# Layer 1's attention on one core: three runs of value products a group for seven, and the side products beside them

## The chip, the core and the metric

The kernel runs on one core of a Trainium2 chip. The metric is device time in microseconds, the median of several runs; lower is better.

## What is computed

Four layers, each a cross attention and then a feed-forward part, on x (8 x 256 x 128) with a context of 8 x 1601 x 128. The change touches layer 1's cross attention alone, 16 heads of width 8:

```python
q = query @ Wq + bq          # query: layernorm(x)
k = key @ Wk + bk            # key, value: the context
v = value @ Wv + bv
scores = jnp.einsum('bqhd,bkhd->bhqk', q, k) * scale
attn = jax.nn.softmax(scores, axis=-1)
out = jnp.einsum('bhqk,bkhd->bqhd', attn, v)
return out.reshape(out.shape[0], out.shape[1], ATTEN_DIM) @ Wo + bo
```

## The kernel before

`build_heads` works in bodies, one for each of the 8 batch elements, and a body in 4 groups of 4 heads (`NG`). The context's 1601 positions are 13 tiles of 128 (`CT`). For a group there are:

- 14 **top** steps (T0 to T13 of a numbering in which 4 to 13 are done one group ahead, as `T`, and 0 to 3 two groups ahead, as `U`): PE multiplies queries and keys (line 454) into a PSUM tile of the ring, and DVE takes maxima over positions (lines 717, 715). Steps 12 and 13 are narrow (66 columns).
- **shift** (`H`), three small operations on DVE that turn the maxima into a row, and **rows** (`W`), a product of PE (line 501) with DVE's addition (line 731): they put the maximum into `shifted`, so that the next group's scores come out less their maximum.
- 13 **score** steps (S0 to S12): PE (line 435) into a ring tile, ACT takes the exponential into `probs` (line 603), which has 8 places (`PS`).
- 7 **value** steps (V0 to V6) of two tiles each, the last of one: PE adds probabilities times values into `res` (line 475), four products of 32 columns a tile, one a head. **Result** (`R`) is ACT's copy of `res` into `oraw` (line 607).

`ring` has 3 tiles of two banks each (`RING`); scores and tops take them in turn, and PE waits for the one three ring steps back to be read. One more bank, `aux`, serves the **side products**, placed by the table `SIDE`: key (line 487, the next body's, copied by ACT at line 617 and subtracted by DVE at 739), value (line 492, the projection of the next body's values, copied by ACT at 625), denominator (line 511), spread (521, read by DVE at 748), project (527) and finish (534) for the body before.

The order of everything is written by hand: `ORDER` is a string with one group's steps, `SIDE` says after which step of which group (0 to 3) a side product stands and for which body, and every engine walks the same list (`run_bodies`) with its own part of each step. Offsets in the list say that a step belongs to the group before or after. A product in 64 rows (scores, tops), one in 128 rows and 32 columns (values) and one in 128 by 128 (`aux`) are three shapes of the array, named 64*128, 128*32 and 128*128 in the trace.

Of the kernel before, what the change touches and what calls it, by code (L numbers as in the profile page):

```python
# [59 lines left out]
class Semaphores:  # L60
# [3 lines left out]
    def __init__(self, nc):  # L64
        self.nc = nc
        self.old, self.now, self.later = [(ExitStack(), []) for _ in range(3)]
# [113 lines left out]
class HeadsPlan:  # L180
# [3 lines left out]
    H, DH, NG, HG = 16, 8, 4, 4  # L184
# [8 lines left out]
    KB = -(-CT // 4)  # L193
    AUX = ("key", "value", "rows", "denominator", "spread", "project", "finish")

    ORDER = """S0 T4 S1 V5 T12 S2 T13 T5 V6 S3 T6 R T7 S4 T8 V0 S5 T9 V1 T10 S6 T11 V2 S7 U0 U1 H S8 S9 V3 U2 S10 W S11 U3 S12 V4"""
    SIDE = {(0, "T4"): ("key", 0, 1), (0, "T7"): ("key", 1, 1), (0, "T9"): ("key", 2, 1), (0, "T11"): ("key", 3, 1),
            (0, "V3"): ("denominator", 0, -1), (1, "S1"): ("spread", 0, -1), (1, "T13"): ("spread", 1, -1), (1, "T6"): ("project", 0, -1),
            (1, "U0"): ("value", 0, 1), (2, "S4"): ("finish", 0, -1), (2, "U0"): ("value", 1, 1), (3, "R"): ("value", 2, 1),
            (3, "U0"): ("value", 3, 1)}  # L200

    def __init__(self):

        self.order = []
        put = lambda kind, n, off=0: self.order.append((kind, off, n))
        for g in range(self.NG):
            of = lambda d: ((g + d) % self.NG, (g + d) // self.NG)
            for s in self.ORDER.split():  # L210
                k = int(s[1:] or 0)
                if s[0] == "S":
                    put("scores", g * CT + k)
                elif s[0] in "TU":
                    G, off = of(1 if s[0] == "T" else 2)
                    put("tops", (G, k), off)
                elif s[0] == "H":
                    put("shift", *of(1))
                elif s[0] == "W":
                    put("rows", *of(1))  # L220
                elif s[0] == "V":
                    G, off = of(-1 if k >= 5 else 0)
                    put("values", G * self.PV + k, off)
                else:
                    put("result", *of(-1))
                if (g, s) in self.SIDE:
                    put(*self.SIDE[g, s])
        self.aux = Numbered(self.order, self.AUX, ("key",))
        self.ring = Numbered(self.order, ("scores", "tops"))
        self.high = Numbered(self.order, ("key",), ("key",))  # L230


def build_heads(nc, held, io, x, x_in, x_out):
    c = HeadsPlan()
# [3 lines left out]
    with ExitStack() as ctx, ExitStack() as done:  # L238
# [56 lines left out]
        aux_full, aux_free, hi_ok, parts_ok = sem("aux_full"), sem("aux_free"), sem("hi_ok"), sem("parts_ok")  # L295
# [245 lines left out]
        def _(act):  # L541
# [62 lines left out]

            def result(b, par, g):
                act.wait_ge(pv_ok, b * NG * c.PV + (g + 1) * c.PV)
                act.activation(oraw[:, g, :], res[:, 0:S], ACT.Copy).then_inc(oraw_ok, 1)  # L607

            def key(b, par, k):
# [18 lines left out]
            def project(b, par, n):  # L628
                full(b, "project")
                act.activation(ft[:, :], aux[:, 0:S], ACT.Identity, bias=bfin[:, 0:1], scale=1.0).then_inc(aux_free, 1)  # L630

            run_bodies(act, c.order, dict(scores=scores, result=result, key=key, value=value, project=project))

        @block.gpsimd
# [127 lines left out]
class MaskedPlan:  # L762
# [3 lines left out]
    H, DH, NP, NR = 16, 64, 8, 16  # L766
# [545 lines left out]
class SelfPlan:  # L1312
# [3 lines left out]
    H, DH, NG = 16, 8, 4  # L1316
# [519 lines left out]
class LatentPlan:  # L1836
# [32 lines left out]
    def put(self, kind, n):  # L1869
        if kind in ("stats", "norm", "scale", "norm_y", "norm_hi", "turn", "turn_lo"):  # L1870
            b = n[0] if isinstance(n, tuple) else n
            if b >= B:
                return
        elif kind not in ("weights", "foldq", "folda", "foldc", "foldv", "foldf", "foldb"):
            u = n[0] if isinstance(n, tuple) else n
            if not 0 <= u < self.NU:
                return
        self.order.append((kind, n))
# [677 lines left out]
G = 4  # L2556
# [1023 lines left out]
```

## Time and profile before

| | |
|---|---|
| median of 3 runs | 4359.4 us (4358.38 to 4363.13) |
| the profiled execution | 4360.64 us |
| its span, first to last instruction | 4358.9 us |
| PE busy in the span | 4044.0 us (93%) |
| DVE busy | 2754.8 us (63%) |
| ACT busy | 2779.4 us (64%) |
| POOL busy | 857.5 us (20%) |
| mean granted TensorE clock | 0.964 of full speed |

PE is TensorE, DVE is VectorE, ACT is ScalarE, POOL is GpSimd. Busy time is an average over stages; layer 1's attention loop lies between 452 and 1090 us of the span. PE's matmuls are pipelined, so that a step's length overlaps the start of the next one: what a step costs is read from start to start.

### The profile page before, as it was taken

What the parts mean: (1) busy time and instruction counts of PE and PEld (TensorE: products, weight loads), DVE (VectorE), ACT (ScalarE), POOL (GpSimd) and SP (SyncE); (2) the same over time, 40 slices, a digit from 0 to 9 for tenths busy, and PEclk for the clock granted to TensorE, in tenths of its full rate; (3) what the DMA queues carried; (4) which work ended last, traced back from release to release, by engine and by line L of the source; (5) the groups of instructions that cost most, each with busy time, mean ns of one, the idle gap of its engine ahead of it and who ended that gap; (6) DMA issues with size and microseconds to landing.
All of it is one profiled execution on the core that took longest, in us unless ns stands there. A gap on an engine that the chain in (4) does not pass through costs nothing. (4 is left out here: it accounts for less than half of the span.)

```text
span 4358.9 us, 72369 instructions
## 1 busy us (share of the span) xinstructions
PE 4044.0 (93%) x26524; PEld 2864.6 (66%) x26524; DVE 2754.8 (63%) x6263; ACT 2779.4 (64%) x4848; POOL 857.5 (20%) x755
## 2 busy tenths in 40 slices
PE   7897999999899999999999999789999999988799
PEld 6654444454477777777777777547888888864467
DVE  7655888887565665556565565465555555548656
ACT  6523667777267666666767666437777777757456
POOL 2100000000000000000000000006777777751200
PEclk9898899999899999999999999899999999989899
DMA  2100433230100000000000000100000000000100
GB/s 73 39 1 29 80 49 47 48 43 10 44 12 13 1 12 1 12 1 13 1 13 12 1 1 1 43 16 9 9 8 9 8 1 1 1 9 1 39 4 8
DMA packets 55897, 78.90 MB, mean 18 GB/s; under 512 B 10164, under 2 KB 47172, under 8 KB 54444
## 3 DMA queue, kind: packets, MB, share of 16 engines
q1 hardware_dynamic: 51084, 67.97, 7.3%
q10 hardware_dynamic: 4464, 6.30, 0.4%
q8 instruction: 216, 3.54, 0.3%
q14 instruction: 133, 1.09, 0.1%
HBM read 51.31 MB, written 4.19 MB: 13 GB/s over the span
## 5 line engine op out<-in xcount | busy, mean ns | idle before, releaser
L2405 POOL TENSOR_TENSOR L3a_p_lo<-L3a_wq,L3a_p_hi 128x512 fp32r<-128x512 f32 (+1 forms) x480 | 623.4, 1310 | 262.9 <-ACT L3a_p_hi L2355 254.5
L1255 DVE CUSTOM_DVE_ANT_0 L2a_sc<-L2a_score,L2a_mask_n 128x804 f32<-128x804 f32 x512 | 498.8, 991 | 212.8 <-issue 199.5
L1145 ACT ACTIVATE L2a_pt<-L2a_ring 128x512 f32<-128x512 f32 x768 | 431.2, 598 | 167.9 <-PE L2a_ring L1034 164.2
L603 ACT ACTIVATE L1a_work<-L1a_ring 128x1024 f32<-128x1024 f32 x416 | 412.4, 1026 | 161.5 <-PE L1a_ring L435 161.4
L717 DVE TENSOR_REDUCE L1a_mx<-L1a_ring 128x2 f32<-128x1024 f32 x384 | 456.3, 1221 | 50.7 <-PE L1a_ring L454 46.2
L1034 PE MATMUL L2a_ring<-L2a_ident,L2a_sc 128*128 128x128 f32 x3072 | 437.2, 280 | 13.2 <-ACT L2a_pt L1145 8.4
L1130 ACT ACTIVATE L2a_sc<-L2a_sc,L2a_nb 128x1608 f32<-128x1608 f32 x256 | 417.1, 1631 | 0.7 <-DVE L2a_nb L1260 0.7
L2493 DVE TENSOR_REDUCE L3a_mx<-L3a_ring 128x1 f32<-128x402 f32 (+2 forms) x640 | 316.2, 537 | 145.3 <-PE L3a_ring L2207 137.6
L1034 PEld LDWEIGHTS L2a_ring<-L2a_ident,L2a_sc 128*128 128x128 f32 x3072 | 339.1, 142 | 90.2 <-issue 40.8
L2354 ACT ACTIVATE L3a_wq<-L3a_ring 128x512 f32<-128x512 f32 (+1 forms) x480 | 283.8, 591 | 159.9 <-PE L3a_ring L2129 102.8
L1049 PE MATMUL L2a_res<-L2a_pt,L2a_v 128*64 128x256 f32 (+1 forms) x3328 | 375.4, 382 | 1.6 <-ACT L2a_pt L1145 1.6
L1278 DVE SCALAR_TENSOR_TENSOR L2a_k_lo<-L2a_ring,L2a_bk,L2a_k_hi 128x402 fp32r<-128x402 f32 x256 | 161.3, 635 | 327.2 <-ACT L2a_k_hi L1171 327.2
L1049 PEld LDWEIGHTS L2a_res<-L2a_pt,L2a_v 128*64 128x64 f32 (+1 forms) x3328 | 234.2, 137 | 135.1 <-issue 22.2
L2355 ACT ACTIVATE L3a_p_hi<-L3a_ring 128x512 fp32r<-128x512 f32 (+1 forms) x480 | 282.1, 588 | 0.0
L1171 ACT ACTIVATE L2a_k_hi<-L2a_ring,L2a_bk 128x402 fp32r<-128x402 f32 x256 | 152.4, 598 | 142.0 <-PE L2a_ring L998 134.2
L475 PE MATMUL L1a_res<-L1a_work,L1a_v 128*32 128x256 f32 (+1 forms) x3328 | 229.8, 391 | 3.3 <-ACT L1a_oraw L607 1.7
L1017 PE MATMUL L2a_score<-L2a_k_hi,L2a_q_hi 64*128 64x402 f32 x1024 | 206.3, 397 | 23.1 <-DVE L2a_mx L1255 23.0
L454 PE MATMUL L1a_ring<-L1a_keys,L1a_queries 64*128 64x512 f32 (+1 forms) x1024 | 200.4, 415 | 16.9 <-DVE L1a_mx L717 14.7
L2249 PE MATMUL L3a_res<-L3a_p_hi,L3a_n_hi 128*128 128x512 f32 (+1 forms) x480 | 191.1, 398 | 16.2 <-POOL L3a_p_lo L2405 16.2
L2127 PE MATMUL L3a_ring<-L3a_q_hi,L3a_kt_hi 128*128 128x512 f32 (+1 forms) x480 | 200.1, 417 | 2.0 <-DVE L3a_q_lo L2506 1.0
L435 PE MATMUL L1a_ring<-L1a_shifted,L1a_keys 64*128 64x512 f32 x832 | 189.4, 461 | 7.7 <-ACT L1a_work L603 6.4
L2129 PE MATMUL L3a_ring<-L3a_q_hi,L3a_kt_lo 128*128 128x512 f32 (+1 forms) x480 | 190.9, 398 | 0.0
(742 smaller groups left out, 8742.8 us busy)
## 6 DMA issues: line engine op xcount, KB each, us to landing
L1a_keys<-L1a_k_hi SPq DMA_DIRECT2D x224, 52.0 KB
L1a_kt<-in_ctx_t SPq DMA_DIRECT2D x8, 800.5 KB, 4.4
L2a_ct<-in_ctx_t SPq DMA_DIRECT2D x8, 800.5 KB, 4.3
L1a_keys<-L1a_k_lo SPq DMA_DIRECT2D x112, 52.0 KB
L0a_cx<-in_ctx SPq DMA_DIRECT2D x16, 320.0 KB, 3.8
L3a_cx<-in_ctx SPq DMA_DIRECT2D x16, 320.0 KB, 3.6
L2a_mask_u<-in_mask SPq DMA_DIRECT2D x16, 200.1 KB, 4.4
L1a_scr_q<-L1a_keys SPq DMA_DIRECT2D x3, 1024.0 KB
```

The lines of the kernel that those rows point to most:

```text
L475: mm = pe.matmul(res[32 * r:32 * r + 32, 0:S], v[0:rows, par, jt, h * c.VE:h * c.VE + 32], probs[0:rows, (par * NU + g * CT + jt) % c.PS, ...
L603: act.activation(probs[:, (par * NU + u) % c.PS, :, :], ring[tile][:, :, :], ACT.Exp).then_inc(tile_free[tile], 1)
L717: dve.tensor_reduce(mx[:, g % 2, hf, one, :, ch], ring[tile][:, :, :], AX, ALU.max).then_inc(tile_free[tile], 1)
L1034: mm = pe.transpose(bank[:, t * P:(t + 1) * P], sc[:, r % 2, g // 3, at:at + P], ident[:, :])
L1049: mm = pe.matmul(res[e * DH:(e + 1) * DH, 0:S], v[0:rows, t, h * DH:(h + 1) * DH], pt[0:rows, t, e, :], start=(t == 0), stop=(t == CT - 1))
L1130: act.activation(sc[:, r % 2, e, :], sc[:, r % 2, e, :], ACT.Exp, bias=nb[:, r % 2, e:e + 1], scale=1.0, accum_out=sums[:, r // 2 % 2, r % ...
L1145: ins = act.activation(pt[:, t:t + 4, g // 3, q], bank[:, :].rearrange("p (t q) -> p t q", t=4), ACT.Copy)
L1255: dve.tensor_tensor_reduce(sc[:, two, e, w].rearrange("p (k j) -> p k j", k=2), score[e][:, :, 0:CH], mask_n[:, r % 2, w].rearrange("p (k ...
L2354: act.activation(probs[0:r, at % 2, 0:W], bank[0:r, 0:W], ACT.Exp)
L2355: free(act.activation(p_hi[0:r, at % PH, 0:W], bank[0:r, 0:W], ACT.Exp), "scores", k)
L2405: pool.tensor_tensor(p_lo[0:r, at % PL, 0:W], probs[0:r, at % 2, 0:W], p_hi[0:r, at % PH, 0:W].bitcast(F32), ALU.subtract).then_inc(part_o ...
L2493: free(dve.tensor_reduce(mx[:, u % 2, part, to:to + 1], bank[:, 0:valid(s, ch)], AX, ALU.max), "tops", k)
```

## The change

`ORDER` and `SIDE` are written anew. V4, V5 and V6 stand together after T6 of the next group (V4 stood at its own group's end), V0 and V1 after T9, V2 and V3 after U1. Most side products stand directly ahead of or behind one of the three runs. The tops of a group keep their number and their tiles, in a slightly different order. V4 belongs to the next group now (`k >= 4`), and ACT waits for the reader of the spread before it writes over `oraw`, since the second spread now stands behind the result.

```diff
-    ORDER = """S0 T4 S1 V5 T12 S2 T13 T5 V6 S3 T6 R T7 S4 T8 V0 S5 T9 V1 T10 S6 T11 V2 S7 U0 U1 H S8 S9 V3 U2 S10 W S11 U3 S12 V4"""
-    SIDE = {(0, "T4"): ("key", 0, 1), (0, "T7"): ("key", 1, 1), (0, "T9"): ("key", 2, 1), (0, "T11"): ("key", 3, 1),
-            (0, "V3"): ("denominator", 0, -1), (1, "S1"): ("spread", 0, -1), (1, "T13"): ("spread", 1, -1), (1, "T6"): ("project", 0, -1),
-            (1, "U0"): ("value", 0, 1), (2, "S4"): ("finish", 0, -1), (2, "U0"): ("value", 1, 1), (3, "R"): ("value", 2, 1),
-            (3, "U0"): ("value", 3, 1)}
+    ORDER = """S0 T4 S1 T12 T5 S2 T6 V4 V5 V6 R S3 T7 S4 T13 T8 S5 T9 V0 V1 S6 T10 S7 T11 H S8 U0 S9 U1 V2 V3 W S10 U2 S11 U3 S12"""
+    SIDE = {(0, "T6"): ("key", 0, 1), (0, "R"): ("key", 1, 1), (0, "T9"): ("denominator", 0, -1), (0, "V1"): ("key", 2, 1),
+            (0, "U1"): ("key", 3, 1), (1, "T6"): ("spread", 0, -1), (1, "R"): ("spread", 1, -1), (1, "T9"): ("project", 0, -1),
+            (1, "V1"): ("finish", 0, -1), (1, "U1"): ("value", 0, 1), (2, "T6"): ("value", 1, 1), (2, "R"): ("value", 2, 1),
+            (2, "T9"): ("value", 3, 1)}
@@
-                    G, off = of(-1 if k >= 5 else 0)
+                    G, off = of(-1 if k >= 4 else 0)
@@
             def result(b, par, g):
                 act.wait_ge(pv_ok, b * NG * c.PV + (g + 1) * c.PV)
+                if b and g % 2 == 0:
+                    act.wait_ge(aux_free, c.aux(b - 1, "spread", g // 2) + 1)
                 act.activation(oraw[:, g, :], res[:, 0:S], ACT.Copy).then_inc(oraw_ok, 1)
```

PE, from a rows product in the end of group 2 of a body into group 3, before (L501 rows, L435 scores, L454 tops, L475 values; each x2 of a ring step is the two halves of one tile, x8 of L475 two tiles of values):

```order
L501 MATMUL L1a_aux<-L1a_ident_b,L1a_parts 128x128 x4
L435 MATMUL L1a_ring<-L1a_shifted,L1a_keys 128x512 x2
L454 MATMUL L1a_ring<-L1a_keys,L1a_queries 128x512 x2
L435 MATMUL L1a_ring<-L1a_shifted,L1a_keys 128x512 x2
L475 MATMUL L1a_res<-L1a_work,L1a_v 32x256 x8
L435 MATMUL L1a_ring<-L1a_shifted,L1a_keys 128x512 x2
L454 MATMUL L1a_ring<-L1a_keys,L1a_queries 128x512 x2
L435 MATMUL L1a_ring<-L1a_shifted,L1a_keys 128x512 x2
L475 MATMUL L1a_res<-L1a_work,L1a_v 32x256 x8
L454 MATMUL L1a_ring<-L1a_keys,L1a_queries 128x66 x4
L435 MATMUL L1a_ring<-L1a_shifted,L1a_keys 128x512 x2
```

Of the change, the same place:

```order
L501 MATMUL L1a_aux<-L1a_ident_b,L1a_parts 128x128 x4
L435 MATMUL L1a_ring<-L1a_shifted,L1a_keys 128x512 x2
L454 MATMUL L1a_ring<-L1a_keys,L1a_queries 128x512 x2
L435 MATMUL L1a_ring<-L1a_shifted,L1a_keys 128x512 x2
L454 MATMUL L1a_ring<-L1a_keys,L1a_queries 128x512 x2
L435 MATMUL L1a_ring<-L1a_shifted,L1a_keys 128x512 x4
L454 MATMUL L1a_ring<-L1a_keys,L1a_queries 128x512 x2
L435 MATMUL L1a_ring<-L1a_shifted,L1a_keys 128x512 x2
L454 MATMUL L1a_ring<-L1a_keys,L1a_queries 128x66 x4
L454 MATMUL L1a_ring<-L1a_keys,L1a_queries 128x512 x2
L435 MATMUL L1a_ring<-L1a_shifted,L1a_keys 128x512 x2
L454 MATMUL L1a_ring<-L1a_keys,L1a_queries 128x512 x2
```

Before, a value run stands after every three ring steps here; of the change twelve ring steps follow one another, and behind them comes L475 x20, the values of five tiles.

PE in group 0 of a body, from S5 on, of the change (L511 is the denominator, L487 a key product):

```order
L435 MATMUL L1a_ring<-L1a_shifted,L1a_keys 128x512 x2
L454 MATMUL L1a_ring<-L1a_keys,L1a_queries 128x512 x2
L511 MATMUL L1a_aux<-L1a_pick,L1a_oraw 128x4 x8
L475 MATMUL L1a_res<-L1a_work,L1a_v 32x256 x16
L487 MATMUL L1a_aux<-L1a_kt,L1a_wk 128x512
L435 MATMUL L1a_ring<-L1a_shifted,L1a_keys 128x512 x2
```

Before, L511 stood behind V3 and this L487 behind T9; now both stand at the run V0 and V1, one on each side.

## Rows read from the trace of the kernel before

**Rows 1.** Windows: start and end, length, busy time (x instructions), clock, DMA
```profile
530.40:1013.06 482.66, 468.53 (x4394) 234.50 (x4393) 414.64 (x481) 344.48 (x444) 11.44 (x6) 0.99 0.31 46
530.40:553.33 22.93, 21.95 (x192) 10.60 (x191) 19.02 (x24) 15.37 (x18) 0.12 (x1) 1.00 0.24 60
553.33:573.57 20.24, 19.87 (x192) 10.77 (x191) 17.38 (x21) 14.14 (x19) 1.79 (x1) 1.00 0.47 58
573.57:591.99 18.42, 17.74 (x176) 8.68 (x177) 16.53 (x20) 13.80 (x19) 0.00 (x0) 1.00 0.49 61
591.99:610.08 18.09, 17.77 (x176) 8.79 (x177) 16.17 (x19) 14.05 (x20) 0.00 (x0) 1.00 0.17 41
714.12:735.88 21.76, 21.39 (x193) 11.25 (x191) 17.38 (x21) 14.20 (x19) 1.79 (x1) 0.92 0.47 58
```
The busy times are PE, PEld, DVE, ACT and POOL in this order.

**Rows 2.** Timeline of PE in a group 3: start, length, instruction, [idle before <-releaser]
```profile
755.41 0.50 PE L454 MATMUL L1a_ring<-L1a_keys,L1a_queries 64*128 64x512 f32 x2 [0.28 <-DVE L1a_mx L717]
...
757.08 0.51 PE L435 MATMUL L1a_ring<-L1a_shifted,L1a_keys 64*128 64x512 f32 x2
757.42 0.40 PE L454 MATMUL L1a_ring<-L1a_keys,L1a_queries 64*128 64x512 f32 x2
757.66 0.39 PE L435 MATMUL L1a_ring<-L1a_shifted,L1a_keys 64*128 64x512 f32 x2
757.98 1.07 PE L475 MATMUL L1a_res<-L1a_work,L1a_v 128*32 128x256 f32 x16
758.98 0.41 PE L454 MATMUL L1a_ring<-L1a_keys,L1a_queries 64*128 64x66 f32 x4
...
760.34 0.64 PE L475 MATMUL L1a_res<-L1a_work,L1a_v 65*32 65x256 f32 x8
760.91 0.50 PE L435 MATMUL L1a_ring<-L1a_shifted,L1a_keys 64*128 64x512 f32 x2
...
761.57 1.16 PE L492 MATMUL L1a_aux<-L1a_wv,L1a_kt 128*128 128x128 f32 x8
762.66 0.50 PE L454 MATMUL L1a_ring<-L1a_keys,L1a_queries 64*128 64x512 f32 x2
```
A float32 product counts twice in the trace, so x16 are the values of two tiles.

**Rows 3.** Timeline of PE at the loop's end
```profile
1087.77 1.50 PE L475 MATMUL L1a_res<-L1a_work,L1a_v 128*32 128x256 f32 x24 [0.43 <-ACT L1a_work L603]
```

**Rows 4.** Timelines of DVE and of ACT in the same group 3
```profile
754.14 1.22 DVE L717 TENSOR_REDUCE L1a_mx<-L1a_ring 128x2 f32<-128x1024 f32 x1
...
757.86 1.23 DVE L717 TENSOR_REDUCE L1a_mx<-L1a_ring 128x2 f32<-128x1024 f32 x1 [0.68 <-PE L1a_ring L454]
...
763.20 8.18 DVE L717 TENSOR_REDUCE L1a_mx<-L1a_ring 128x2 f32<-128x1024 f32 x7 [0.29 <-PE L1a_ring L454]
...
757.63 1.94 ACT L603 ACTIVATE L1a_work<-L1a_ring 128x1024 f32<-128x1024 f32 x2 [0.41 <-PE L1a_ring L435]
```

**Rows 5.** Timeline of PE, side products in other groups
```profile
703.72 1.12 PE L487 MATMUL L1a_aux<-L1a_kt,L1a_wk 128*128 128x512 f32 x2
704.78 1.07 PE L475 MATMUL L1a_res<-L1a_work,L1a_v 128*32 128x256 f32 x16
...
711.58 1.95 PE L511 MATMUL L1a_aux<-L1a_pick,L1a_oraw 128*128 128x4 f32 x16
...
719.37 0.66 PE L521 MATMUL L1a_aux<-L1a_ident,L1a_rq_wide 128*128 128x128 f32 x4
...
723.99 1.99 PE L527 MATMUL L1a_aux<-L1a_on,L1a_wfin 128*128 128x256 f32 x8
...
744.53 0.44 PE L534 MATMUL L1a_aux<-L1a_ident,L1a_ft 128*128 128x128 f32 x2
```

**Rows 6.** Timelines of ACT and of DVE: a key product's two readers
```profile
701.50 0.69 ACT L617 ACTIVATE L1a_k_hi<-L1a_aux,L1a_bk 128x512 fp32r<-128x512 f32 x1 [0.57 <-PE L1a_aux L487]
...
705.61 0.75 DVE L739 SCALAR_TENSOR_TENSOR L1a_k_lo<-L1a_aux,L1a_bk,L1a_k_hi 128x512 fp32r<-128x512 f32 x1 [0.37 <-ACT L1a_k_hi L617]
```

**Rows 7.** Windows: the stretch after a denominator, columns as in rows 1
```profile
715.90:719.30 3.40, 3.40 (x24) 1.42 (x22) 1.31 (x2) 1.83 (x3) 0.01 (x1) 0.51 0.53 68
```

## The prediction

> **What bounds the kernel now.** First I asked which stretch the change touches. The windows show layer 1's attention main loop, 8 bodies of 4 groups, from 452.1 to 1089.7 us; the six full bodies take 482.66 us, 80.4 each, with PE busy 97%, DVE 86%, ACT 71% at a granted clock of 0.99 [rows 1]. The four kinds of group take 22.93, 20.24 (21.76 in another body), 18.42 and 18.09 us [rows 1]: what differs is how many side products they hold. Nothing outside this loop is edited.
>
> Second, PE's timeline inside a group without stalls gives the price of a step from start to start [rows 2]. Between two steps of its kind a score or top step takes 0.24 us (757.42 to 757.66); the last before a value run 0.32 to 0.33 (757.66 to 757.98); the first after one 0.34 (757.08 to 757.42). A value pair of two tiles takes 1.00 (757.98 to 758.98), of one tile 0.57 (760.34 to 760.91). So a tile costs 0.43 and a run 0.14 beside it; a run of three tiles at the end of the loop is 1.50 long against 1.07 for two, again 0.43 more [rows 3]. One run and the two changes around it cost 0.14 + 0.09 + 0.10 = 0.33 us that no product needs. The change attacks this.
>
> Third, the other side of the ring. A tile holds until ACT's exponential (1.02 long, 0.92 apart in a row: 1.94 for two) or DVE's maximum (1.22 long; seven in 8.18, so 1.16 apart; 1.14 where they stand closest) has read it [rows 4]. The reader starts 0.44 after the start of a product within a run (757.42, read at 757.86) and 0.55 after that of the first one (757.08, read at 757.63) [rows 2, 4]. PE reuses a tile 0.05 after the read: the maximum begun at 754.14 ends at 755.36 and PE starts at 755.41, after waiting [rows 2, 4]. With three tiles, one trip of a tile is 0.44 + 1.02 + 0.05 = 1.51 us (score) or 1.71 (top), so 27 ring steps need at least about 9 trips, 14.4 us, **if the tiles never rest**. They rest, and both readers go idle, once a value run outlasts what three tiles hold. Today a run of 1.00 stands after every two to four ring steps and fits behind the readers' backlog: of the 18.09 us PE is busy 17.77.
>
> **The change, part by part.** *Merged runs.* A group has three runs (5, 4 and 4 tiles) for seven. PE's list has 222 value runs before and 96 after, and 669 changes between products of the three shapes before, 317 after. 126 x 0.14 + 352 x 0.095 = 51 us less work on PE. That is the gain if PE's work is the bound.
>
> *What is late next: the ring.* I walk a group without side products with the rules above. After the run V4 to V6 (0 is the start of S3): S3 0, T7 0.34, S4 0.57; both readers are idle and start at 0.58 (behind the copy of the result) and 0.78. T13 needs S3's tile: 0.58 + 1.07 = 1.65. T8 needs T7's: 0.78 + 1.27 = 2.05. S5 needs S4's, whose exponential starts at 1.50: 2.57. T9 2.80, and V0 starts at 3.13. So 7 steps that are 1.7 us of products take 3.13. V0, V1: 4 x 0.43 + 0.14 = 1.87. DVE has T8's and T9's maxima until 4.85, then idles until T10 is there: about 0.9. After that run: S6 0, T10 0.34, S7 0.57, T11 1.62, S8 2.05, U0 2.54, S9 3.33, U1 3.57, run at 3.90 (the three small operations of the shift keep DVE 0.7 between T11 and U0). V2, V3 1.87, then the rows product 0.33. Then the long stretch: S10 0, U2 0.34, S11 0.57, U3 1.62, S12 2.14, S0 2.54, T4 3.33, S1 3.65, T12 4.57, T5 5.04, S2 5.49, T6 5.72, run at 6.05. V4 to V6: 5 x 0.43 + 0.14 = 2.30. Sum: 3.13 + 1.87 + 3.90 + 1.87 + 0.33 + 6.05 + 2.30 = **19.45 us**. The same kind of group takes 18.09 today [rows 1], and that with two value projections in it. So +1.35.
>
> *Side products beside the runs.* Before, they stand mostly between ring steps, where readers' backlog partly hides them. Behind or ahead of a run they lengthen a stop in which the tiles already rest, so I charge them in full, each 0.06 to 0.08 less than the length shown, since the next step starts before the last end (a key product is 1.12 long and takes 1.06, 703.72 to 704.78): key 1.06 (the last one, a quarter as wide, 0.42), denominator 1.87, each spread 0.59, projection of the output 1.92, value projection 1.09 (761.57 to 762.66), the last of four 0.42, final turn 0.37 [rows 2, 5]. A key product right behind a run costs more: ACT copies it (0.69) and DVE subtracts (0.75) ahead of the next maximum in DVE's order [rows 6]. The maximum of T7 or T10 then starts at 1.49 and not 0.78; walked on, the next run starts 0.43 later after V6 and 0.70 later after V1. A value projection behind V6 delays ACT by its four copies: 0.23.
> Group 0: 19.45 + 3 x 1.06 + 0.42 + 1.87 + 0.43 + 0.70 = 26.0 (now 22.93). Group 1: 19.45 + 1.17 + 1.92 + 0.37 + 1.09 = 24.0 (now 20.24 or 21.76). Group 2: 19.45 + 2.18 + 0.42 + 0.23 = 22.3 (now 18.42). Group 3: 19.45 (now 18.1). A body: 91.8 against 80.4, **+11.3**, times six = +68. Body 0 has no run V4 to V6 in its first group, no denominator, spread or projection: 0, +2.4, +4.2 and +1.35, some +8. The last has no keys or projections for a next body and fewer tops; by the same sums its groups are +1.5, +1.6, +1.1 and +1, +5.
>
> *The added wait* on ACT, before the copy of groups 0's and 2's results: the spread's reader on DVE stands behind T6's maximum, done about 2 us after the run began, and the copy can't start before the run's end plus the second spread. Cost nothing; were the cover gone, DVE's 0.69 for it would be the price, once a body, 5 us. The key rows for the next body start their DMA some 8 us later in the body; their first reader is a group 2's U0, over 40 us on, and none waits in these windows. Nothing.
>
> The profiled execution took 4360.6 us (span 4358.9 and 1.7 around it), 1.2 above the median of the three. 4360.6 + 68 + 8 + 5 = **4442 us**, 1.9% slower.
>
> **Rule against row.** The trace prices a change of product shape at about 0.095 us a side and 0.14 for a value run [rows 2]. The Trainium skill, TensorEngine Tiling (Array Packing), Key Properties, says that changing the tiling mode drains TensorE; the rows agree that a change costs something. By that rule alone fewer changes are a pure gain, and it speaks for the change.
>
> **Rivals.** (1) *PE's work is the bound, not the ring.* For it: PE busy 97% today. Against: that busy time contains waits for tiles already (rows with "<-DVE L1a_mx", [rows 2]), and the merged runs raise the readers' idle time from 0.68 after one run to 0.9 or 1.3 after each. It decides if readers keep up, that is if reuse of a tile took under about 1.3 us and not 1.5 to 1.7. Then 4360.6 - 51 = 4310 us, **faster**. 7%. (2) *Gains and stalls cancel*, since side products still hide behind the readers' backlog and the ring loses less: within 0.2% (9 us, about what a measurement of this kernel can tell), 4361 us. 5%. (3) *Only part of the loss*: side products hidden three quarters (9.4 of 12.6 us), 4361 + 6 x 1.9 + 8 = 4380. 4%. (4) *The clock falls too.* At 715.9 it stood at 0.51, its lower level 1.2 GHz, for 3.4 us, shortly after PE had run the denominator's narrow products and waited; that group took 21.76, where the one with the clock at 1.00 took 20.24: 1.5 us a fall [rows 1, 7]. Now PE waits for tiles before every run and the denominator follows such a stretch. One fall more a group is 32 x 1.5 = 48: 4490 us. 14%. The Trainium skill, TensorE: Matmul & The Clock Gate, Part 1, says that the slow clock is the default and activity releases it; the fall at 715.9 agrees in kind.
>
> **How the numbers follow.** The forecast has 70%. Its own uncertainty: if half of the side products' 12.6 us a body stay hidden, 6 x 6.3 = 38 less, 4404; the upper end is the fourth case, 4490. This takes in forecast and clock case, 84%. Slower: 70 + 14 + 4 = 88%; same 5%; faster 7%.
>
> **What would show it.** Right: group 3 near 19.4 us, group 0 near 26, body near 92; value runs of 2.3 and 1.87 us; DVE idle about 1 us after each, ended by L1a_ring tops; ACT's and DVE's busy time in the loop unchanged; PE's idle time waiting for L1a_mx and L1a_work much larger. Wrong: group 3 under 18 us with PE steps 0.24 apart; or side products before a run that leave the body's length alone. If the clock is much below 0.99 in 530 to 1100 us, case four.

## The result and the profile after

| | before | after |
|---|---|---|
| median | 4360.4 us | 4544.4 us (4541.8 to 4555.7) |
| ratio | | 1.0424 (95%: 1.0411 to 1.0437) |
| profiled execution, its span | 4358.9 us | 4553.9 us |
| mean granted TensorE clock | 0.964 | 0.943 |

The change is slower by 184 us. The forecast was 4442 (4404 to 4490), 81 us slower: the direction was right, the size less than half. One execution of a later run (e1_fill) took some 100 us longer than its others at a lower clock, and its profile is not used.

The windows of the changed kernel: first the six full bodies, then the four groups of one body (0, 1, 2, 3), then the whole loop. Columns as in [rows 1].

```profile
555.99:1186.56 630.57, 537.77 (x4396) 283.94 (x4394) 416.54 (x481) 345.67 (x444) 11.43 (x6) 0.88 0.23 34
...
973.75:1006.51 32.76, 27.83 (x194) 13.86 (x192) 19.28 (x24) 15.24 (x18) 1.91 (x1) 0.79 0.04 13
1006.51:1033.90 27.39, 23.94 (x193) 13.31 (x194) 17.99 (x21) 14.41 (x19) 0.00 (x0) 0.88 0.46 56
1033.90:1059.58 25.68, 21.83 (x189) 12.10 (x186) 16.22 (x18) 14.79 (x23) 0.00 (x0) 0.87 0.34 42
1059.58:1079.52 19.94, 16.49 (x168) 8.34 (x168) 15.90 (x18) 13.15 (x14) 0.00 (x0) 0.99 0.01 2
457.45:1275.57 818.12, 696.44 (x5752) 363.64 (x5752) 534.87 (x615) 455.37 (x574) 13.34 (x7) 0.87 0.23 34
```

The loop takes 818 us where it took 637.6 (452.1 to 1089.7): +180.5 of the 195 us between the two profiled executions; the other 14.5 lie in stages that the change does not touch, where the clock is a little lower (0.92 for 0.93 ahead of the loop, 0.96 for 0.97 behind it); why, nothing here shows. A full body takes 105.1 us for 80.4. DVE and ACT do the same work as before (416.5 for 414.6 us, 345.7 for 344.5), so that what grew is time in which they stand idle. Of the 148 us that six bodies are longer, PE is busy for 69 more (537.8 for 468.5, with the same products) and idle for 79 more, and the clock is 0.88 where it was 0.99 [rows 1]. Half clock for a share s of the time gives a mean of 1 - s/2. With the clock unrounded (0.8755 and 0.9894), 157 of the 630.57 us passed at 1.2 GHz, against 10 of 482.66.

The timeline of PE in a group 3 shows the ring's part; it begins at S10 behind the rows product. This group has no side product now, where the one before had two value projections, 1.5 us of PE's time.

```profile
954.19 0.50 PE L435 MATMUL L1a_ring<-L1a_shifted,L1a_keys 64*128 64x512 f32 x2
954.53 0.40 PE L454 MATMUL L1a_ring<-L1a_keys,L1a_queries 64*128 64x512 f32 x2
954.77 0.40 PE L435 MATMUL L1a_ring<-L1a_shifted,L1a_keys 64*128 64x512 f32 x2
955.82 0.49 PE L454 MATMUL L1a_ring<-L1a_keys,L1a_queries 64*128 64x512 f32 x2 [0.65 <-ACT L1a_work L603]
956.26 0.98 PE L435 MATMUL L1a_ring<-L1a_shifted,L1a_keys 64*128 64x512 f32 x4
957.64 0.50 PE L454 MATMUL L1a_ring<-L1a_keys,L1a_queries 64*128 64x512 f32 x2 [0.40 <-DVE L1a_mx L719]
...
960.37 2.37 PE L475 MATMUL L1a_res<-L1a_work,L1a_v 128*32 128x256 f32 x40
962.67 0.49 PE L435 MATMUL L1a_ring<-L1a_shifted,L1a_keys 64*128 64x512 f32 x2
```

Three steps go out in 0.58 us, and then PE waits for the first tile's exponential: U3 starts 1.63 after S10 (walked: 1.62), T4 at 3.45 (3.33), the run at 6.18 (6.05). The run takes 2.30, as walked. Behind the runs the readers stand still, as DVE's timeline shows (the first line behind V4 to V6, the second behind V0 and V1):

```profile
963.43 1.23 DVE L719 TENSOR_REDUCE L1a_mx<-L1a_ring 128x2 f32<-128x1024 f32 x1 [1.07 <-PE L1a_ring L454]
...
968.50 1.23 DVE L719 TENSOR_REDUCE L1a_mx<-L1a_ring 128x2 f32<-128x1024 f32 x1 [0.88 <-PE L1a_ring L454]
```

Over the six bodies the groups of instructions (busy, mean | idle before) show the same; first before, then after.

```profile
L717 DVE TENSOR_REDUCE L1a_mx<-L1a_ring 128x2 f32<-128x1024 f32 x289 | 343.8, 1221 | 35.7 <-PE L1a_ring L454 31.8
...
L454 PE MATMUL L1a_ring<-L1a_keys,L1a_queries 64*128 64x512 f32 (+1 forms) x768 | 147.4, 406 | 8.9 <-DVE L1a_mx L717 7.4
```

```profile
L719 DVE TENSOR_REDUCE L1a_mx<-L1a_ring 128x2 f32<-128x1024 f32 x289 | 346.5, 1222 | 86.9 <-PE L1a_ring L454 85.6
...
L454 PE MATMUL L1a_ring<-L1a_keys,L1a_queries 64*128 64x512 f32 (+1 forms) x768 | 159.8, 435 | 79.1 <-ACT L1a_work L603 59.2 <-DVE L1a_mx L719 18.0
```

PE's idle time ahead of top products went from 8.9 to 79.1 us, and what ends it is a tile being read.

The second part shows in group 0. PE's timeline, and the windows of two stretches at half clock in it:

```profile
977.46 0.50 PE L454 MATMUL L1a_ring<-L1a_keys,L1a_queries 64*128 64x512 f32 x2 [0.41 <-DVE L1a_mx L719]
...
980.87 2.07 PE L487 MATMUL L1a_aux<-L1a_kt,L1a_wk 128*128 128x512 f32 x2
982.87 3.25 PE L475 MATMUL L1a_res<-L1a_work,L1a_v 128*32 128x256 f32 x40
...
989.87 0.50 PE L454 MATMUL L1a_ring<-L1a_keys,L1a_queries 64*128 64x512 f32 x2 [0.60 <-DVE L1a_mx L719]
...
990.76 2.90 PE L511 MATMUL L1a_aux<-L1a_pick,L1a_oraw 128*128 128x4 f32 x16
993.59 3.64 PE L475 MATMUL L1a_res<-L1a_work,L1a_v 128*32 128x256 f32 x32
997.16 1.70 PE L487 MATMUL L1a_aux<-L1a_kt,L1a_wk 128*128 128x512 f32 x2
```

```profile
977.90:984.70 6.80, 6.52 (x36) 2.78 (x36) 4.76 (x5) 3.29 (x4) 0.00 (x0) 0.50 0.00 0
991.60:998.40 6.80, 6.80 (x44) 3.86 (x44) 1.52 (x3) 0.07 (x1) 1.91 (x1) 0.50 0.00 0
```

Each of the two falls begins after PE has waited for tiles, and then the value run and the side products, the one work that TensorE does at a stretch, pass at 1.2 GHz: 3.25 for 2.37 us, 3.64 for 1.94, a key product 2.07 for 1.12. In the second stretch PE feeds the ring nothing, and DVE is busy for 1.52 us of 6.80 and ACT for 0.07.

The same waits do not bring a fall each time. Two groups 3 of two other bodies, with the same instructions:

```profile
745.56:765.48 19.92, 16.47 (x171) 8.32 (x167) 15.87 (x18) 13.15 (x14) 0.00 (x0) 0.99 0.00 1
849.56:872.49 22.93, 19.49 (x170) 9.31 (x167) 16.75 (x19) 13.15 (x14) 0.00 (x0) 0.85 0.00 1
```

In the second the clock falls, and it takes 3.0 us longer. What decides between the two, no run here shows.

### The profile page after: what moved, and what is told of

Read it like the earlier page. It is cut to its first block and busy times, and to the rows that moved or that the text cites. A ratio compares the mean times of both kernels' runs of the same rounds, so it can differ in the third digit from the quotient of the medians.

```text
span 4553.9 us, 72383 instructions
## 1 busy us (share of the span) xinstructions
PE 4136.6 (91%) x26524; PEld 2930.3 (64%) x26524; DVE 2757.4 (61%) x6263; ACT 2779.7 (61%) x4848; POOL 855.2 (19%) x755
## 3 DMA queue, kind: packets, MB, share of 16 engines
q14 instruction: 133, 1.09, 0.1%
## 5 line engine op out<-in xcount | busy, mean ns | idle before, releaser
L454 PE MATMUL L1a_ring<-L1a_keys,L1a_queries 64*128 64x512 f32 (+1 forms) x1024 | 216.0, 443 | 103.1 <-ACT L1a_work L603 74.4
L475 PE MATMUL L1a_res<-L1a_work,L1a_v 128*32 128x256 f32 (+1 forms) x3328 | 241.6, 442 | 0.7 <-ACT L1a_work L603 0.7
L454 PEld LDWEIGHTS L1a_ring<-L1a_keys,L1a_queries 64*128 64x128 f32 x1024 | 100.6, 204 | 187.6 <-ACT L1a_work L603 128.1
L435 PE MATMUL L1a_ring<-L1a_shifted,L1a_keys 64*128 64x512 f32 x832 | 197.0, 474 | 18.6 <-DVE L1a_mx L719 14.3
```

What stands on the lines that cost most here:

```text
L454: mm = pe.matmul(ring[tile][:, t, k * w:(k + 1) * w], queries[half_of(t), par, g, e, hf * P:(hf + 1) * P], keys[half_of(t), par, g, ch * C ...
```

## The experiments

Theory A: two causes, the ring's stops (as walked) and the clock falls they bring. B: the stops alone. C: TensorE's own work is the bound and the walk is wrong. The expectations also speak of a switch theory (what counts is the changes of shape that are saved) and a ring theory (what counts is how long the tiles feed their readers).

In the diffs, @@ stands for lines left out.

**Fillers where PE waits.** Products whose result nobody reads are put where PE waits for a ring tile. F3 in `ORDER` is three of them, 64 rows by 512 columns, written to the spare bank `aux`; F3b is the same and left out in group 0; G3 is six of half the width, written beside `res`. The lines that are added to the changed kernel:

```diff
+    ORDER = """S0 F2 T4 S1 F3 T12 F1 T5 S2 T6 V4 V5 V6 R S3 T7 S4 G3 T13 T8 S5 T9 V0 V1 S6 T10 S7 F3b T11 H S8 U0 F2 S9 U1 V2 V3 W S10 U2 S11 F3 U3 S12"""
@@
+                elif s[0] == "F":
+                    if g or s[2:] != "b":
+                        put("fill", (g, len(self.order), int(s[1])))
+                elif s[0] == "G":
+                    put("fill_res", (g, int(s[1])))
@@
+            def filler(bank, par, g, n):
+                for _ in range(n):
+                    pe.matmul(bank, queries[0:64, par, g, 0, 0:P], keys[0:64, par, g, 0:bank.shape[-1]], start=True, stop=True)
+            def fill(b, par, n):
+                pe.wait_ge(aux_free, c.both(b, "fill", n) - c.fills(b, "fill", n))
+                filler(aux[:, :], par, n[0], n[2])
@@
+                pe.wait_ge(oraw_ok, b * NG + n[0])
+                filler(res[:, S:2 * S], par, n[0], 2 * n[1])
```

> The changed kernel with 17 filler products of 64 rows x 512 columns a group (14 in group 0), placed where TensorE waits for a ring tile; they go to columns nobody reads, so the output is the same. Theory A, two causes (the ring's stops, and clock falls that these stops bring about): nearly no half-clock stretch is left in the loop, group 3 stays near 19.5 to 20, a full body falls from 105 to about 92 to 94, the kernel to 4445 to 4465 us. Theory B, the stops alone cost and the slow clock only fills time that would be waited anyway: the clock rises, the body stays near 105, 4540 us. Theory C, TensorE's own work is the bound: the fillers add 17 x 0.21 x 32 = 115 us, 4660 us.

It took 4476.3 us (1.0266 times the kernel before, 95%: 1.0249 to 1.0283), above the 4445 to 4465 of theory A. The same kernel ran again for its profile:

> The same kernel as e1_fill, whose one profile fell in a disturbed execution; wanted is its profile. 4476 us again; half-clock stretches in the loop about 30 to 60 us for the changed kernel's 207, a full body 94 to 96 us, group 3 near 20 without a fall.

4470.8 us (1.0253, 1.0234 to 1.0271): 74 us less than the changed kernel, though it does more. Windows: six bodies, then groups 0 to 3 of one, then a group 0 of another body.

```profile
548.25:1118.08 569.83, 552.80 (x4858) 321.18 (x4856) 415.10 (x481) 345.71 (x444) 11.44 (x6) 0.99 0.26 38
```
```profile
927.35:956.03 28.68, 26.17 (x211) 14.23 (x209) 19.11 (x24) 15.25 (x18) 1.91 (x1) 0.94 0.05 15
956.03:980.40 24.37, 24.28 (x213) 14.66 (x214) 18.00 (x21) 14.41 (x19) 0.00 (x0) 1.00 0.46 54
980.40:1003.08 22.68, 22.22 (x207) 13.40 (x206) 15.81 (x18) 14.79 (x23) 0.00 (x0) 1.00 0.46 58
1003.08:1022.90 19.82, 19.71 (x189) 11.23 (x188) 16.28 (x19) 13.15 (x14) 0.00 (x0) 1.00 0.00 1
833.74:860.44 26.70, 24.57 (x212) 13.79 (x208) 19.19 (x24) 15.25 (x18) 1.90 (x1) 1.00 0.05 16
```

The clock is back at 0.99 (17 us at half clock in six bodies for 157), and a body takes 95.0 us for 105.1. B and C fall: useless products bought time. What is left, 19.82, 22.68 and 24.37 us for groups 3, 2 and 1, is 0.4 above the walk each (19.45, 22.3, 24.0). Group 0 takes 28.68 with the clock at 0.94, and 26.70 in the one body in which the clock stays up, 0.7 above its walk (26.0).

This also gives a price: 10.1 us a body for 23.3 us less at half clock, 0.43 us for each us.

**Side products alone.** The kernel before with another `SIDE`, nine of the thirteen side products of a body directly beside one of its seven runs:

```diff
+    SIDE = {(0, "V5"): ("key", 0, 1), (0, "T8"): ("key", 1, 1), (0, "T9"): ("key", 2, 1), (0, "T11"): ("key", 3, 1),
+            (0, "V3"): ("denominator", 0, -1), (1, "S1"): ("spread", 0, -1), (1, "T5"): ("spread", 1, -1), (1, "T8"): ("project", 0, -1),
+            (1, "V2"): ("value", 0, 1), (2, "T8"): ("finish", 0, -1), (2, "V2"): ("value", 1, 1), (3, "V6"): ("value", 2, 1),
+            (3, "V2"): ("value", 3, 1)}
```

> The kernel before, ORDER untouched, with nine of the thirteen side products of a body moved directly beside one of the seven value runs. Switch theory: nine round trips of 0.19 us less a body, 8 x 1.7 = 14 us less, 4346 us. Ring theory: a stop of 1.0 + 1.1 us outlasts the readers' backlog by about 0.5 us each time, 8 x 4 = 32 us more less the 14, 4375 to 4385 us, and a few more clock falls.

4412.7 us (1.0123, 1.0106 to 1.0140), worse than either theory said. Windows of six bodies and of a group 3, and the longest wait of PE in that group:

```profile
535.10:1063.44 528.34, 484.68 (x4395) 240.96 (x4394) 416.51 (x481) 345.67 (x444) 11.44 (x6) 0.95 0.28 41
1044.04:1063.44 19.40, 17.69 (x179) 8.86 (x178) 16.32 (x19) 14.18 (x20) 0.00 (x0) 1.00 0.00 1
...
1053.60 0.51 PE L435 MATMUL L1a_ring<-L1a_shifted,L1a_keys 64*128 64x512 f32 x2 [0.90 <-ACT L1a_work L603]
```

Group 3, with the same two value projections moved beside V6 and V2, goes from 18.09 to 19.40 with the clock at 1.00: 1.3 us more for two moved products, which should have saved two round trips of 0.19. The wait of 0.90 stands at the fourth ring step behind V6 and its projection. The switch theory of side products is gone.

**Runs alone.** The changed kernel with side products between ring steps:

```diff
+    SIDE = {(0, "T4"): ("key", 0, 1), (0, "S4"): ("key", 1, 1), (0, "T10"): ("key", 2, 1), (0, "S8"): ("denominator", 0, -1),
+            (0, "S11"): ("key", 3, 1), (1, "T12"): ("spread", 0, -1), (1, "S4"): ("spread", 1, -1), (1, "T10"): ("project", 0, -1),
+            (1, "S8"): ("finish", 0, -1), (1, "S11"): ("value", 0, 1), (2, "T4"): ("value", 1, 1), (2, "S4"): ("value", 2, 1),
+            (2, "T10"): ("value", 3, 1)}
```

> The changed kernel's ORDER with its three value runs, but the side products between ring steps. Theory A: the side products fill TensorE's waits for tiles, most of their 12.6 us a body disappears, a body takes 81 to 86 us with fewer half-clock stretches, 4375 to 4420 us. If the long runs alone make the loss, it stays near 4540 us. If the runs alone are the gain, it is below 4330 us.

4467.8 us (1.0247, 1.0231 to 1.0262), 48 us above the span that theory A gave. A body takes 93.3 us and not 81 to 86: a side product fills a wait of PE, and it seems to push back a step that its reader then has to wait for, which is argued here and not shown. Group 3 holds two stretches of 3.4 us at half clock:

```profile
549.67:1109.71 560.04, 489.26 (x4397) 258.01 (x4394) 413.98 (x480) 343.47 (x444) 11.45 (x6) 0.94 0.26 39
899.23:922.00 22.77, 19.32 (x170) 9.27 (x168) 16.69 (x19) 13.16 (x14) 0.00 (x0) 0.85 0.19 44
```

The same with fillers in group 3 and at the end of group 2 (the condition is `if g == 3 or g == 2 and s[2:] == "b"`, and F3b stands behind S11 now):

> e3_runs (three value runs, side products between ring steps) with fillers at TensorE's waits in group 3 and at the end of group 2, where no side product stands. Its group 3 took 21.4 to 23.0 us with a half-clock stretch in each. If stops and clock falls add up: group 3 goes to 19.7 to 20.0 us, a body from 93.3 to about 90, the kernel from 4468 to 4435 to 4450 us; what is left over the kernel before is the ring's part of the three runs. If the fall only moves to another group, the time stays near 4468 us.

4450.9 us (1.0205, 1.0188 to 1.0223), and group 3 without a fall:

```profile
543.55:1092.83 549.28, 501.61 (x4535) 275.01 (x4532) 413.84 (x481) 343.25 (x444) 11.43 (x6) 0.97 0.27 40
891.20:911.03 19.83, 19.73 (x190) 11.24 (x188) 16.28 (x19) 13.15 (x14) 0.00 (x0) 1.00 0.22 53
```

19.83 for 22.77 us in a group, 0.43 us for each us at half clock again. The kernel as a whole lies 1 us above what was expected, and a body takes 91.5 us and not about 90; the other groups kept their falls (0.97).

The four ways, in us a body. Beside each stands how much of it passed at half clock (from the unrounded granted clock of the six bodies), and what is left when 0.43 us is taken off for each us of that:

| | side products between steps | beside the runs |
|---|---|---|
| seven runs | 80.4, 1.7 at half clock; 79.7 (before) | 88.1, 8.0 at half clock; 84.6 (e2_side) |
| three runs | 93.3, 10.8 at half clock; 88.6 (e3_runs) | 105.1, 26.2 at half clock; 93.7 (the change) |

Without the clock, three runs cost about 9 us a body in either column, and side products beside the runs about 5 in either row. With it, the two together cost 24.7 where the single ones add to 20.6 (7.7 and 12.9): what the combination costs beyond its parts is clock, 9.1 us more at half clock than the parts add to, or 3.9 us of the 4.1.

**Half the reading.** Both kernels with half of the maxima and half of the probabilities left out; the scale on the exponential changes values only:

```diff
-                                       probs[0:rows, (par * NU + g * CT + jt) % c.PS, r // 2, r % 2 * S:(r % 2 + 1) * S],
+                                       probs[0:rows, (par * NU + g * CT + jt) % c.PS, r // 2, 0:S],
@@
-                act.activation(probs[:, (par * NU + u) % c.PS, :, :], ring[tile][:, :, :], ACT.Exp).then_inc(tile_free[tile], 1)
+                act.activation(probs[:, (par * NU + u) % c.PS, :, 0:S], ring[tile][:, :, 0:S], ACT.Exp, scale=0.01).then_inc(tile_free[tile], 1)
@@
-                    dve.tensor_reduce(mx[:, g % 2, hf, one, :, ch], ring[tile][:, :, :], AX,
+                    dve.tensor_reduce(mx[:, g % 2, hf, one, :, ch], ring[tile][:, :, 0:S], AX,
```

> The changed kernel with the readers' work halved: exponentials and maxima read 256 of the 512 columns of each half tile, so half of the maxima and half of the probabilities are left out (the value products take the first half twice). TensorE's work is the same. Ring theory: a trip of a tile falls from 1.5 to 1.7 us to about 1.1, the walk of a group 3 gives 16.1 us for 19.45, a body about 78.5 with the clock up: 4335 us with no clock falls left, up to 4437 us with all of them. Switch theory (TensorE bound either way): no change beyond 1%.

> The kernel before with the same halved reads as e4_short_after (half of the maxima and of the probabilities left out). If its loop is bound by TensorE's own steps, as its 17.77 us of busy time in a group of 18.09 say, it gains at most 0.3 to 0.7 us a group: 4338 to 4352 us, where the changed kernel gained 176. If the readers bind both kernels, it gains about as much as the changed one, below 4250 us.

The changed kernel fell by 176 us to 4368.2 (1.0014, 1.0005 to 1.0023), the kernel before by 29 to 4331.0 (0.9928, 0.9910 to 0.9946). Windows of six bodies and of a group 3; the changed kernel first.

```profile
526.59:1022.96 496.37, 458.07 (x4395) 253.42 (x4394) 264.18 (x480) 216.47 (x444) 11.44 (x6) 0.98 0.31 46
1006.22:1022.96 16.74, 15.46 (x169) 8.25 (x168) 9.94 (x18) 7.72 (x14) 0.00 (x0) 1.00 0.12 14
```
```profile
521.31:982.82 461.51, 453.27 (x4395) 233.47 (x4394) 270.00 (x481) 216.25 (x444) 11.44 (x6) 0.99 0.34 50
965.83:982.82 16.99, 16.92 (x179) 8.70 (x178) 10.14 (x19) 8.71 (x19) 0.00 (x0) 1.00 0.10 12
```

PE has the same products to do, so the ring's trips, with the clock falls that they bring, were the changed kernel's price. The kernel before was bound by PE with a larger share of the readers than I had said: it gained 7 us more than the range's 8 to 22, and 1.1 us of its 18.09 in a group 3 are the readers', not 0.3 to 0.7. PE's busy time there fell from 17.77 to 16.92 us with the same products, so 0.85 us of it seem to have been waits that the profile counts as busy.

Even with short reads three runs do not win. A body takes 82.7 us for 76.9. The two groups 3, 16.74 and 16.99 us, do not hold the same work: the second holds two value projections, for which the prediction charges 1.09 and 0.42 us, and the first none. Without them the kernel before would stand at about 15.5 us, an estimate from these numbers. So the 4 x 0.33 = 1.3 us of saved switches do not come to light even here.

**How long may a run be?** The kernel before with V5 moved back behind S2 and V6 moved up to it, and with V0 moved back beside V1:

```diff
+    ORDER = """S0 T4 S1 T12 S2 V5 V6 T13 T5 S3 T6 R T7 S4 T8 V0 S5 T9 V1 T10 S6 T11 V2 S7 U0 U1 H S8 S9 V3 U2 S10 W S11 U3 S12 V4"""
+    ORDER = """S0 T4 S1 V5 T12 S2 T13 T5 V6 S3 T6 R T7 S4 T8 S5 T9 V0 V1 T10 S6 T11 V2 S7 U0 U1 H S8 S9 V3 U2 S10 W S11 U3 S12 V4"""
```

> The kernel before with V6 (one tile) moved up to V5: one run of 1.43 us once a group for one of 1.00 and one of 0.57. Switch price: 0.33 us less TensorE work a group, 4350 us. The readers' backlog there is 1.2 to 1.6 us, so the ring theory lets it pass or takes 0.1 to 0.3 us a group back: 4350 to 4362 us. No more clock falls than before.

> The kernel before with V0 and V1 together behind T9: one run of 1.87 us a group for two of 1.00. Ring theory: a stop 0.4 to 0.9 us beyond the backlog, less 0.33, so 0.3 to 0.6 us more a group, plus a fall or two more in a body: 4375 to 4400 us. Switch theory: 4350 us.

The first, three tiles in one run, took 4392.5 us (1.0068, 1.0052 to 1.0084), 30 more than its range's upper end; the second, four tiles, 4381.5 (1.0048, 1.0031 to 1.0065), as the ring theory said. Both are slower than the kernel before, by 0.7 and 0.5%. The first miss is instructive. The edit also took the value run out from between S1 and T12, so five ring steps stood in a row, and PE waits there, not behind the run:

```profile
769.35 0.40 PE L454 MATMUL L1a_ring<-L1a_keys,L1a_queries 64*128 64x512 f32 x2
769.58 0.40 PE L435 MATMUL L1a_ring<-L1a_shifted,L1a_keys 64*128 64x512 f32 x2
770.63 0.41 PE L454 MATMUL L1a_ring<-L1a_keys,L1a_queries 64*128 64x66 f32 x4 [0.65 <-ACT L1a_work L603]
```

Before, the run V5 stood in this place and no wait was to be seen. Where PE would have to wait anyway, a value run fills the wait. I had looked at the run's length and forgotten the place it left. The wait is 0.65 of the 1.1 us that a group 3 of this kernel is longer (19.2 for 18.1, with the clock at 1.00); where the rest lies is not shown.

**The denominator.** Five falls are left in the six bodies of e1b_fill, all in group 0: four begin at the denominator's end, one some 24 us into the group. Now a wide product follows all but the last of the denominator's eight. Diff against e1_fill:

```diff
                         mm = pe.matmul(aux[:, at:at + 4], oraw[:, g, hf * P:(hf + 1) * P], pick[:, :], start=True, stop=True)
+                        if n == 0 and not (isinstance(b, int) and b == B - 1) and (hf, g) != (SH - 1, NG - 1):
+                            pe.matmul(res[:, S:2 * S], keys[:, 1 - par, 0, 0:P], keys[:, 1 - par, 0, 0:S], start=True, stop=True)
```

> e1_fill with a wide product of 256 columns behind seven of the denominator's eight products of 4 columns, written where nobody reads. In e1b_fill the half-clock stretches that are left lie at the denominator of group 0. If its narrow products bring them: at most one is left in six bodies, group 0 falls from 28.3 to 26 to 27.5 us though the step itself is 0.7 to 1.5 us longer, the kernel 4460 to 4475 us. If the falls come from the waits ahead of it, they stay and the kernel takes 4480 us or more.

4482.4 us, and over the six bodies:

```profile
548.36:1124.36 576.00, 559.83 (x4900) 328.19 (x4898) 415.34 (x481) 346.23 (x444) 11.43 (x6) 0.98 0.26 38
```

The falls stayed, seven of 3.4 us for five. In four of the six bodies they moved, though: the clock stays up over the denominator and falls 24 us into the group, behind two more waits of PE. In one of these bodies:

```profile
756.50:762.00 5.50, 5.50 (x59) 3.91 (x57) 2.49 (x3) 1.02 (x1) 1.91 (x1) 1.00 0.05 18
766.30:769.70 3.40, 3.40 (x22) 1.60 (x26) 2.94 (x6) 1.67 (x3) 0.00 (x0) 0.50 0.01 2
...
764.00 0.50 PE L475 MATMUL L1a_ring<-L1a_keys,L1a_queries 64*128 64x512 f32 x2 [0.80 <-ACT L1a_work L626]
765.01 0.50 PE L456 MATMUL L1a_ring<-L1a_shifted,L1a_keys 64*128 64x512 f32 x2 [0.51 <-DVE L1a_mx L742]
```

So group 0 keeps a fall with the denominator's work filled up, and its narrow products are not shown to bring it. The waits of group 0 that hold no filler are the likelier cause; that is not tested, and why the fall moved stays open.

No kernel tried beats the kernel before, except that kernel itself with half the reading left out.

## Why the prediction was right or wrong

*What bounds the kernel.* Right in kind: PE's work, with the ring close behind. How close was underrated (1.1 us of 18.09).

*Merged runs save work on PE.* The value runs came out as walked (2.30 us for five tiles), but the saving came out as waiting, even with half the reading. What the saved changes of shape are worth by themselves, no run shows.

*The ring walk.* Right: 19.45 us for a group 3, measured 19.94 with the clock at 0.99 and 19.82 with fillers. The 0.4 us lie in the three stretches of ring steps, 6.18, 3.19 and 4.10 us for 6.05, 3.13 and 3.90 walked; the runs took what was walked.

*Side products in full.* Right: 24.0 and 22.3 us walked for groups 1 and 2, 24.37 and 22.68 measured with the clock up, and 26.0 for group 0, 26.70 measured. These are totals of a group; no run tests a single charge by itself. Of the body's loss about 5 us belong to the place of the side products and 9 to the three runs, as the table of the four ways shows.

*The sum.* The ring and the side products make +87 us in six bodies (569.83 less 482.66, fillers in), for +68 forecast. About 11 of these 19 us are what the four groups take above their walk with the clock up, the rest the five falls that the fillers left. The whole kernel with fillers is 110 us slower than the kernel before, for 81 forecast.

*The clock.* This is the step that failed: the sum holds the clock at its old level and puts nothing for it. It stood as rival (4), 14%, 4490 us: one fall more a group. The fillers put it at 74 us at least, of the 102 by which the forecast was short. The price of rival (4) was right: 157 us at half clock in six bodies against 17 with fillers cost 10.1 us a body, 0.43 us for each us at half clock, and 3.4 us of it 1.5. Its count was wrong: 24.5 us more at half clock in a body than before are seven times 3.4 us, not four, and no body was spared. I had the row that shows one fall after a single stretch of waits [rows 7], I made PE wait in more than seven places a group in my own walk, and still put the sum at an unchanged clock. Forecast and rival (4) are not alternatives: in e1b_fill most of the falls go with the waits, so the second follows from the first. The other 29 us short are the sum's, the 110 for 81 above. The range missed by 54 us because its upper end took rival (4) with its count and no error of the walk on top.

*The added wait, the keys' DMA.* Put at nothing, and nothing in the traces speaks against it: the copy of the result waits for PE's value products, and group 3 holds its walked length.

*Rivals (1) to (3).* (1) fell by e1b_fill and e4_short_after, (2) and (3) by the result. Against (1) the prediction put waits inside PE's busy time, but the rows named for it show idle time ahead of PE, 0.28 us in the group; that such waits exist, some 0.85 us in a group 3, is read from e5_short_before alone.

## What to carry to other kernels

Before products are put together to spare changes of shape, walk the ring: how long do its tiles feed the readers, and does PE wait already where the run stood? With three tiles and reads of 1.0 to 1.2 us, runs of 1.0 us after every two to four steps left PE idle for 0.3 us of 18.09, one run of 1.9 us in their place cost 0.8 us in a group 3 (18.9 us in e7_v01), and five steps in a row cost a wait of 0.65. Where a walk makes TensorE wait in many places, charge the clock too, from the start: here it fell to half for just the work that comes in one piece. And before two groups are compared, count what each of them holds.

## What was not expected of the hardware

The clock stood at its lower level for 157 of 630.57 us while the profile showed PE busy for 537.8 of them, and waiting for a ring tile for no more than 0.9 us at a time. Fillers in 64 of the array's 128 rows, 0.23 us apart, put in those waits, brought it to 17 of 569.83. So products that compute nothing were worth 74 us in a kernel that was already 184 us too slow, which is a diagnosis and not a remedy.
